# Two places in a 1-core transformer kernel: integers turned in two stages, and an MXFP4 feed-forward spread over three points of a unit

## The reference

```python
x = x + L0_xattn(layernorm(x), ctx)   # windowed attention, window 16, 8 heads
x = x + L0_ffn(layernorm(x))          # int8 SwiGLU: rows quantized to integers
x = x + L1_xattn(layernorm(x), ctx)   # 32 heads, 8 kv heads of 128, rms norm
x = x + L1_ffn(layernorm(x))          # MXFP4: blocks of 32 share a power of two
x = x + L2_xattn(layernorm(x), ctx)   # 32 heads of 16
x = x + L2_ffn(layernorm(x))          # top 16 of 64 low-rank experts
x = x + L3_xattn(layernorm(x), ctx)   # 16 heads, 4 kv heads of 96
x = x + L3_ffn(layernorm(x))          # 3-bit weights
```

## Time and profile before

| | before |
|---|---|
| time, median of 3 runs | 1607.87 us (1606.4 to 1609.18) |
| time of the profiled execution | 1607.15 us |
| span, first to last instruction | 1605.4 us |
| mean granted TensorE clock | 0.990 |
| PE busy | 1534.7 us (96%) |
| PEld busy | 1279.3 us (80%) |
| DVE busy | 836.7 us (52%) |
| ACT busy | 762.0 us (47%) |
| POOL busy | 519.2 us (32%) |

### The profile page before, as it was taken

The page is one execution under the profiler, slowest core; times in us unless marked ns, Lnnn a source line. Parts: engine busy times, 40 slices in busy tenths (PEclk is TensorE's granted clock), DMA queues, the critical chain, the costliest instruction groups (busy, mean ns, idle before and its releaser), DMA issues. The chain is left out here.

```text
span 1605.4 us, 26173 instructions
## 1 busy us (share of the span) xinstructions
PE 1534.7 (96%) x9596; PEld 1279.3 (80%) x9602; DVE 836.7 (52%) x1719; ACT 762.0 (47%) x2551; POOL 519.2 (32%) x648
## 2 busy tenths in 40 slices
PE   8999998899999999999999998878999999999998
PEld 6877887788989888888888897655666687888876
DVE  4666777454344555454444437677566421343465
ACT  4555454445455455445454564445444312455552
POOL 7667772322222222222221223334222000124324
PEclk9999999999999999999999999989999999999999
DMA  8000001011010101001010110001010001123101
GB/s 249 9 8 8 8 2 41 27 60 40 27 40 27 40 27 40 27 1 40 27 40 27 40 53 1 0 30 53 1 40 1 4 27 49 35 77 82 47 26 63
DMA packets 44415, 58.06 MB, mean 36 GB/s; under 512 B 25472, under 2 KB 32656, under 8 KB 41472
## 3 DMA queue, kind: packets, MB, share of 16 engines
q1 hardware_dynamic: 43872, 56.05, 11.2%
q10 hardware_dynamic: 352, 0.34, 0.1%
q0 software_dynamic: 64, 0.00, 0.0%
HBM read 48.77 MB, written 2.10 MB: 32 GB/s over the span
## 5 line engine op out<-in xcount | busy, mean ns | idle before, releaser
L1844 ACT ACTIVATE big<-pb 128x128 f32<-128x128 f32 x384 | 106.5, 277 | 306.8 <-PE pb L883 199.1
L2214 POOL TENSOR_TENSOR big<-big 128x512 f32<-128x512 f32 x96 | 100.0, 1042 | 257.4 <-DVE big L1476 257.4
L1893 ACT ACTIVATE big<-pb,big 128x128 f32<-128x128 f32 x384 | 135.8, 367 | 63.4 <-issue 40.2
L1471 DVE TENSOR_REDUCE big<-pb 128x4 f32<-128x512 f32 x96 | 65.9, 686 | 182.3 <-PE pb L922 174.7
L898 PE MATMUL pb<-wkh,CXh 128*128 128x256 f32 x512 | 149.9, 293 | 0.0
L2204 POOL TENSOR_SCALAR big<-big 128x6 f32<-128x6 f32 x64 | 12.9, 201 | 417.7 <-ACT big L1844 417.4
L898 PE MATMUL pb<-wkl,CXh 128*128 128x256 f32 x512 | 145.2, 283 | 0.0
L898 PE MATMUL pb<-wkh,CXl 128*128 128x256 f32 x512 | 144.3, 282 | 0.0
L1261 DVE TENSOR_TENSOR X<-X,pb 128x512 f32<-128x512 f32 x128 | 86.8, 678 | 76.2 <-PE pb L1109 39.2
L949 PE MATMUL pb<-woh,oh 128*128 128x512 f32 x256 | 111.9, 437 | 5.4 <-DVE X L1261 5.0
L883 PE MATMUL pb<-wqh,CXh 128*128 128x512 f32 x256 | 101.9, 398 | 4.5 <-DVE big L1441 3.1
(11 more groups left out here) (284 smaller groups left out, 3998.9 us busy)
## 6 DMA issues: line engine op xcount, KB each, us to landing
big<-in_w SPq DMA_DIRECT2D x17, 1024.0 KB, 5.0
big<-in_w SPq DMA_DIRECT2D x24, 256.0 KB, 3.0
big<-in_w SPq DMA_DIRECT2D x8, 512.0 KB, 3.6
o<-o SPq DMA_DIRECT2D x96, 32.0 KB, 1.9
X<-in_x SPq DMA_DIRECT2D x8, 256.0 KB, 4.9
big<-in_cn SPq DMA_DIRECT2D x8, 256.0 KB, 2.7
CXlf<-in_cT SPq DMA_DIRECT2D x8, 256.0 KB, 4.9
big<-in_wa SPq DMA_DIRECT2D x1, 2048.0 KB, 8.1
```

What stands on the lines that cost most here:

```text
L1471: v.tensor_reduce(m[j % 2], quarters(bank(p)), AX, MAX, negate=True).then_inc(S.m, 1)
L1844: y = a.activation(sq[i % 2], bank(p)[:, j * width:j * width + 128], ACT.Square, accum_out=ss[i % 2][:, first + j:first + j + 1])
L1893: y = a.activation(e_[:, c], bank(p)[:, c], ACT.Exp, bias=m[j % 2][:, k:k + 1], scale=1.0, accum_out=z[j % 2][:, k:k + 1])
L2214: g.tensor_tensor(quarters(e_), quarters(e_), bc(r[j % 2], 128), MUL).then_inc(*on.to(S.pn))
```

## The change

Layer 0. `f0_turn` is split: `f0_turn` t keeps the gate's integers, which go to bank 7 instead of bank 0, and a new stage `f0_turn_u` t turns the up's integers (bank 3) after the next `l0_out`, one stage later (for tiles 6 and 7 directly behind `f0_turn`, in the banks of before). `l1_turn` t-1 (for t from 1 to 5) moves from ahead of `f0_turn` t to behind `f0_gate` t, into bank 5.

```diff
     def queries_at(u):
-        return {1: [2, 3], 2: [4], 3: [5], 4: [6], 5: [7], 6: [8], 7: [9], 8: [10], 9: [11], 10: [12, 13],
-                12: [14, 15]}.get(u)
+        return [u + 3] if 1 <= u < 13 else None
...
-    ffn1 = pipeline([2 * t for t in range(NT)], [(s, None if s == "f1_wait" else every) for s in f1], ("f1_quant",))
+    ffn1 = pipeline([3 * t for t in range(NT)], [(s, None if s == "f1_wait" else every) for s in f1])
...
+        sides = {64: [(l2_kv, 0)], 65: [(l2_kv, 0), (l2_kv, 9)], 66: [(l2_kv, 0)]}.get(step, [])
-        if step < 60:
+        if step < 59:
             together(stages)
-        elif step < 64:
-            together(stages, (ffn1, 3), (ffn1, 6))
...
+        elif step == 59:
+            together(stages, (ffn1, 9))
         else:
-            together(stages, (ffn1, 0), (l2_kv, 0), (ffn1, 9))
+            together(stages, *sides, (ffn1, 3), (ffn1, 8), (ffn1, 9))
...
             if name == "ffn1":
-                if step == 1:
-                    order.extend(("l2_q", j) for j in range(2))
-                run(1, ffn1)
+                for k in range(3):
+                    run(1, ffn1)
+                    if step == 0 and k < 2:
+                        order.extend([("l2_q", 2 * k), ("l2_q", 2 * k + 1)])
...
+    for t in range(NT):
+        k = order.index(("f0_turn", t)) + 1
+        if t < NT - 2:
+            k += [s for s, _ in order[k:]].index("l0_out") + 1
+        order.insert(k, ("f0_turn_u", t))
+        if 0 < t < NT - 2:
+            order.remove(("l1_turn", t - 1))
+            order.insert(order.index(("f0_gate", t)) + 1, ("l1_turn", t - 1))
...
     if stage == "f0_turn":
-        return [("g", (0 if i < NT - 2 else 5,)), ("u", (3,))] if i < NT - 1 else [("g", (4,)), ("u", (6,))]
+        return [("g", (7 if i < NT - 2 else 5 if i < NT - 1 else 4,))]
+    if stage == "f0_turn_u":
+        return [("u", (3 if i < NT - 1 else 6,))]
...
+    if stage == "l1_turn" and i < NT - 3:
+        return [("p", (5,))]
...
     if stage == "f1_turn":
-        return [("p", (3,) if i < 5 else sh)]
+        return [("p", (3,) if i < 6 else sh)]
     if stage == "f1_mm":
-        return [("p", (7,) if i < 5 else sh)]
+        return [("p", (5,) if i < 6 else sh)]
     if stage == "l2_turn":
-        return [("p", (2,) if i < 3 else sh)]
+        return [("p", (2,) if i < 5 else sh)]
...
             def f0_turn(t):
                 on.wait_ge(S.qg, t + 1)
                 turn_ints(PSUM["f0_turn", t, "g"], xg0, 4)
+
+            def f0_turn_u(t):
                 on.wait_ge(S.qu, t + 1)
-                turn_ints(PSUM["f0_turn", t, "u"], xu0, 4)
+                turn_ints(PSUM["f0_turn_u", t, "u"], xu0, 4)
...
-            def f2_split(j):
-                x, hi, lo = f2_parts(j)
-                on.wait_ge(S.f2h, j + 1)
-                v.tensor_tensor(lo, x, hi.bitcast(F32), SUB).then_inc(S.f2l, 1)
...
+            def f2_split(j):
+                x, hi, lo = f2_parts(j)
+                on.wait_ge(S.f2h, j + 1)
+                on.wait_ge(*on.last)
+                g.tensor_tensor(lo, x, hi.bitcast(F32), SUB).then_inc(*on.to(S.f2l))
```

More of the change, by code:

```diff
@@ L844, in f0_gate @@
                 on.wait_ge(p.free, p.n)
-                for k, (name, q, lo) in enumerate((("g", qgT, wgl), ("u", quT, wul))):
-                    turned = PSUM["f0_turn", t, name]
+                for k, (turned, q, lo) in enumerate(((PSUM["f0_turn", t, "g"], qgT, wgl), (PSUM["f0_turn_u", t, "u"], quT, wul))):
                     on.wait_ge(turned.free, turned.n + 1)
@@ L1209, in tensor_program @@
             do = dict(l0_bias=l0_bias, l0_qk=l0_qk, l0_project=l0_project, l0_scores=l0_scores, l0_turn=l0_turn,
-                      l0_weigh=l0_weigh, l0_out=l0_out, f0_turn=f0_turn, f0_gate=f0_gate, f0_turn2=f0_turn2, f0_down=f0_down,
+                      l0_weigh=l0_weigh, l0_out=l0_out, f0_turn=f0_turn, f0_turn_u=f0_turn_u, f0_gate=f0_gate, f0_turn2=f0_turn2, f0_down=f0_down,
                       l1_q=l1_q, l1_k=l1_k, l1_b=l1_b, l1_s=l1_s, l1_t=l1_t, l1_v=l1_v, l1_d=l1_d, f1_turn=f1_turn, f1_mm=f1_mm,
@@ L1672, in vector_program @@
                       l1_b=l1_b, l1_s=l1_s, l1_z=l1_z, l1_v=l1_v, l1_d=l1_d, f1_quant=f1_quant,
-                      f1_mm=f1_mm, l2_a=l2_a, l2_s=l2_s, l2_z=l2_z, l2_v=l2_v, l2_c=l2_c, f2_split=f2_split, f2_a=f2_a, f2_h=f2_h,
+                      f1_mm=f1_mm, l2_a=l2_a, l2_s=l2_s, l2_z=l2_z, l2_v=l2_v, l2_c=l2_c, f2_a=f2_a, f2_h=f2_h,
                       f2_o=f2_o, l3_begin=l3_begin, l3_keys=l3_keys, l3_values=l3_values, l3_main=l3_main, l3_q=l3_q, l3_a=l3_a, l3_z=l3_z, l3_v=l3_v, l3_c=l3_c, f3_mm=f3_mm)
@@ L1816, in f0_turn, with f0_turn_u @@
                 ints(PSUM["f0_turn", t, "g"], qgT, 512)
-                ints(PSUM["f0_turn", t, "u"], quT, 512)
+            def f0_turn_u(t):
+                ints(PSUM["f0_turn_u", t, "u"], quT, 512)
             def f0_gate(t):
@@ L2077, in scalar_program @@
             do = dict(begin=begin, l0_bias=l0_bias, l0_qk=l0_qk, l0_project=l0_project, l0_scores=l0_scores, l0_turn=l0_turn,
-                      l0_weigh=l0_weigh, f0_split=f0_split, f0_quant=f0_quant, f0_quant_u=f0_quant_u, f0_quant2=f0_quant2, f0_turn=f0_turn, f0_gate=f0_gate, f0_turn2=f0_turn2, l0_ctx=l0_ctx, l1_begin=l1_begin, l1_keys=l1_keys, l1_q=l1_q, l1_k=l1_k,
+                      l0_weigh=l0_weigh, f0_split=f0_split, f0_quant=f0_quant, f0_quant_u=f0_quant_u, f0_quant2=f0_quant2, f0_turn=f0_turn, f0_turn_u=f0_turn_u, f0_gate=f0_gate, f0_turn2=f0_turn2, l0_ctx=l0_ctx, l1_begin=l1_begin, l1_keys=l1_keys, l1_q=l1_q, l1_k=l1_k,
                       l1_b=l1_b, l1_s=l1_s, l1_t=l1_t, l1_v=l1_v, l1_d=l1_d, f1_turn=f1_turn, l2_kv=l2_kv,
@@ L2172, in f0_norm @@
                 if t:
-                    turned = PSUM["f0_turn", t - 1, "u"]
+                    turned = PSUM["f0_turn_u", t - 1, "u"]
                     on.wait_ge(turned.full, turned.n + 1)
@@ L2286, in pool_program @@
             do = dict(begin=begin, l0_bias=l0_bias, l0_norm=l0_norm, l0_mask=l0_mask, l0_sum=l0_sum, l0_ctx=l0_ctx, f0_norm=f0_norm,
-                      f0_silu=f0_silu, f0_down=f0_down, l1_k=l1_k, l1_z=l1_z, f1_quant=f1_quant, l2_begin=l2_begin, l2_a=l2_a, l2_z=l2_z,
+                      f0_silu=f0_silu, f0_down=f0_down, l1_k=l1_k, l1_z=l1_z, f1_quant=f1_quant, l2_begin=l2_begin, l2_a=l2_a, l2_z=l2_z, f2_split=f2_split,
                       l3_z=l3_z, l3_c=l3_c, f3_mm=f3_mm)
```

## The result

The changed kernel takes 1612.44 us (median of 13 runs, 1608.52 to 1615.48), the one before, run beside it, 1608.61 (1606.4 to 1610.54). The ratio is 1.0023, with a 95% interval of 1.0014 to 1.0031: 3.7 us slower where 6.3 us faster was forecast. The profiled execution of the changed kernel took 1615.48 us (span 1613.7), that of before 1607.15 (1605.4).

A forecast was written before the change was run, and what follows sets the result against it. PE was taken to bound the kernel, so only its idle time and slow clock could be won. 1607.15 less 2.0 (layer 0) and 5.0 (layers 1 to 2), plus 0.72 to the median, gave 1600.9 us; range 1593 to 1610.

The forecast's parts named there:

- The clock: Layers 1 to 2: idle groups of 4 to 5 us slow PE's clock; one dip's price, 2.8 us, taken off the gain.
- the drawing: Timeline of the new order in layers 1 to 2 at full clock: `l2_s` 7 at 1112.1, gain 7.8 us.
- What bounds the kernel: PE bounds the kernel; a gain or loss before 1118 moves the end by the same amount.
- Layer 0: One bank wait replaces another; tile 0 gains 0.5, the clock 1.5: 2.0 us, bounds 0 to 3.5.
- The clock's term: Layer 0, tiles 1 and 2: one of two clock dips gone, 1.5 us, bounds 0 and 3.1.
- The loop of layers 1 to 2: Four engines set the pace, 14.8 us between quantisation ends, shorter in last tiles; eight ends from 972.5 to 1062.
- the bound of three: Layers 1 to 2, lower bound: three clock dips, 8.4 us, and another 1 us in four loops, giving -4.6.
- The shared port: GpSimd's `f2_split` subtractions could hold VectorE 0.7 us a time, up to 5 us in eight; left out of the sum.
- The order's gain: Layers 1 to 2: new order gains 5.0 us, with `f2_split` counted as 1.3 us more per GpSimd step.
- (2): Rival, slower: early `f1_turn` waits and lateness feeds on itself, six steps of 2 us more, 1613; chance 0.15.
- (1): Rival, no change: waits replaced by equal ones, layer 1's drained end not made good, 1606 to 1608; chance 0.19.
- The range: Whole kernel: 1593 to 1610 us, leaving out the worse half of the slower rival.

The follow-up runs named there:

- kernel 11: Changed kernel with TensorE's waits in layers 1 and 2 partly filled by useless transposes and GpSimd's bias additions of tiles 0 to 3 ahead of the quantisations: 1601.98 us, 0.9962.
- kernel 12: Changed kernel with only the partial filling of TensorE's waits (none ahead of `f1_turn` 1 to 3), bias additions left over the quantisations: 1603.46 us, 0.9976.
- kernel 7: Kernel before, its order in layers 1 and 2 kept, plus the layer 0 edit and `f2_split`'s subtractions moved to GpSimd: 1598.95 us, 0.9940.
- kernel 6: Changed kernel with `f1_turn` (and `l2_rows`, `f1_norm`, `l2_turn` with it) back behind `l1_s`: 1607.64 us, 1.0000.
- kernel 9: Changed kernel with longer transpose filling ahead of each wait-prone `f1_turn` and most `l2_turn`s, and bias additions of tiles 0 to 3 ahead of the quantisations: 1605.61 us, 0.9983.
- kernel 5: Changed kernel with the longer transpose filling ahead of `f1_turn` and most `l2_turn`s, nothing else changed: 1605.70 us, 0.9984.

## Why the prediction was wrong

Two terms failed. The clock was taken at one dip, 2.8 us, and cost 7.6 to 9.0. Quantisations held by GpSimd were left out, and cost 3.2 us in the chain. Without both (kernel 11) the changed kernel is faster than before, but by less than the drawing said; and the gain comes from layer 0 and from `f2_split`, not from the order.

**What bounds the kernel: right.** Whatever was won or lost by `l2_s` 7 came out at the end unchanged: after is 10.4 us late there and 8.3 at the end, and the 2 us between them are the `l2_q` (1.9) that before had still to do, as counted.

**Layer 0: mechanism right, size low.** The wait changed places, as drawn, with times within 0.3 us. The clock's term was mis-sized: 1.5 taken, 3.1 the bound; both tiles gained, 3.5 together. Forecast 2.0; the experiments say 1.8 to 4.7.

**The loop of layers 1 to 2: the drawing was right up to the last quantisation, at full clock and with an undisturbed VectorE.** The ends of the eight quantisations, forecast (less the 2.0 of layer 0) against kernel 11 and after:

| tile | 0 | 1 | 2 | 3 | 4 | 5 | 6 | 7 |
|---|---|---|---|---|---|---|---|---|
| forecast | 970.5 | 984 | 999 | 1014 | 1027 | 1039 | 1049.5 | 1060 |
| kernel 11 | 970.8 | 984.2 | 998.9 | 1013.5 | 1026.9 | 1038.6 | 1049.9 | 1060.9 |
| after | 975.6 | 991.9 | 1007.5 | 1022.9 | 1036.3 | 1048.5 | 1060.7 | 1074.6 |

With the two faults taken out the loop runs to within 1 us of the forecast in every tile. Behind it the drawing was 3.2 us too short: `l2_s` 7 comes at 1113.3 instead of 1110.1. Of these, 2.0 are there at `l2_s` 1 (1073.0 instead of 1071.0, with 1.2 us of waiting for ScalarE's exponentials), and 1.2 come from the pace behind it (40.3 us instead of 39.1). That kernel 11's time, 1602.0, lies 1.1 us from the forecast's 1600.9 is therefore partly luck. At full clock the forecast's own sum was 2.0 + 7.8, that is 1598.1, and the 2.8 taken off for a dip that kernel 11 does not have made up for the 3.2. The two terms set beside the drawing that failed:

1. *The clock.* "I take one such price off": 2.8 us, while the bound of three, 8.4, stood in the range's working. The measured price is 9.0 us, 7.6 by the ratios, 8.0 in the profiles from `l1_q` 61 on (kernel 12). The price of one was about right (2.3 us behind the stretch from 974.6), their number was not: there were five stretches, three of 6.8 us and two of 3.4. PE was busy for 23.0 us of the 27.2, so an estimate of the work's delay is half of that, 11.5; 8.0 came out at `l2_s` 7. So some of it did land "where PE waits anyway", as I had written, but most did not, since `l1_k` and `f1_mm` behind PE's waits feed the next turn of the loop. The idle groups of 4 to 5 us were in the drawing, and I had tied a price to one of them only.
2. *The shared port.* The row with 1.16 us instead of 0.42 was read, priced at up to 5 us, and left out because layer 2's heavy operations read PSUM. That looked for the partner in the wrong place: not `f2_split` but the bias additions, the very ones of the earlier trace rows, which in the new order fall on five of eight quantisations (on one in before). They cost 3.2 us in the chain. Moving those of four tiles gave 4.2 to 4.8 us alone, since it also spared some of the slow clock, and 1.5 to 2.3 by the times (3.2 in the profiles) once the clock was held. The holding itself agrees with the Trainium skill, "SBUF — State Buffer", section "Who interferes with whom": an operation of VectorE in a two-port mode and one of GpSimd take turns, and here the second ended 0.28 us after GpSimd's did.

**The order's gain was credited to the wrong part.** I took `f2_split` for a load on GpSimd only, 1.3 us a step, and costed VectorE's relief at nothing. It is what gains (5.0 us in the old order, 9.0 in the new): VectorE no longer stands 5.6 to 8.9 us in front of ScalarE's copies, nor does it do the 5.5 us of subtractions. The pace from `l2_s` 1 to 7 was forecast well, 39.1 us against 40.3, with the relief in it. In before's order the same move shortens that stretch too, from 54.3 us to 47.5. Had I drawn that drawing for before's order with the move, the order's own worth would have shown: kernel 7 is even 3.0 us under kernel 11 (3.5 by the ratios; the intervals just touch), though kernel 7 still has 6.8 us at 1.2 GHz and one held quantisation.

**The rivals.** (2) came true in its direction, and that its 1613 lies so near 1612.4 is luck. It asked for 2 us more than drawn in each of six steps. Measured from one quantisation's end to the next, the seven are 2.9, 0.5, 0.4, 0.4, 0.2, 1.7 and 3.4 us longer than drawn; only the first (16.4) passes the 16 that it said decides. `f1_turn` a step early was right in kind (kernel 6 gives back 3.7 us), but what made it late was the clock and the held instruction, not the sum of the loop. Nor did lateness feed on itself: against kernel 12 it was carried unchanged, 2.3 us, from tile 1 to tile 4. The evidence that I set against it, seven loops of 13.3 us before, was none: there PE came to `f1_turn` 10 us after the quantisation's end in tile 0 and never stood waiting for it.

(1) had the right mechanism for what is left: the drained end of layer 1 is not made good. Counted from `l1_q` 61, kernel 11 is 12.0 us behind kernel 7 at `l2_s` 0 and still 5.5 behind at `l2_s` 7, of which the `l2_q` done sooner pays back 1.9. In after this was covered by the other losses.

The range, 1593 to 1610, was too narrow above. Its own lower bounds, 0 for layer 0 and -4.6 for layers 1 and 2, already give 1612.5 from the 1607.87 of before; and with the clock's bound (5.6 more) and the port's 5 set on the forecast it would have reached 1611 to 1612.

## What to carry to other kernels

TensorE's idle time in a loop can cost twice: itself, and the slow clock on the matmuls behind it (in after, 8.0 us for five dips). Where the same engines' next turn hangs on those, give every dip a price and not only one, and then ask of each whether a wait takes it up. Before crediting an order with a gain, price the smaller edits that come with it in the old order, above all what stands in front of them in an in-order queue. When a corrected kernel meets the forecast, add up the forecast's sum without the terms that this kernel does not have, before taking it as proof. When a row shows an instruction held by another engine, look in the new order for every place where that same pair can meet.

## What the runs showed of the hardware

- Filling idle time with useless transposes, nine times with 0.8 to 2.9 us, made a kernel 9.0 us faster (kernel 12; 7.6 by the ratios). Filling 1.7 to 3.1 us too much in three tiles hid what the earlier additions gave (kernel 9).
- The filling was transposes only, and the clock stayed at its 2.4 GHz level through it and behind it (1.00 in kernel 5's stretch, with 3.08 us of transposes in tile 0). The Trainium skill, "TensorE: Matmul & The Clock Gate", section "Part 4: PE-mode transpose", says that the full clock does not engage for transposes; these runs don't agree, for transposes among matmuls.
- The same kernel's runs differ, and the clock with them: after took 1608.5 us in the runs with a mean clock of 0.992 and 1615.5 in that with 0.986. Its profiled execution was its slowest; from `l0_scores` 29 to 30 it took 12.7 us, where kernel 5, with the same instructions up to there, took 11.1. So part of what a single pair of profiles shows (8.3 us) is chance; the ratio says 3.7. Of the 12.5 us between the profiles of after and kernel 12, 4.4 stand ahead of `l1_q` 61, where both have the same instructions.
- VectorE's 128x512 int32 operation from SBUF to SBUF took 0.42 us by itself and up to 1.35 while GpSimd added two 128x512 f32 tiles (1.28).
